# Local attention: the mask laid down by four products of 64 rows each, and GpSimd adding the halves of the squares

## The reference

```python
def local_attention(q, k, v):          # windows of 64 tokens, each looks at itself and the one before
    ...
    sim = jnp.einsum('bhwid,bhwjd->bhwij', bq, bk)          # bq is q * 8
    mask = (i < j) | (i > j + WINDOW) | (j == -1)
    sim = jnp.where(mask, -jnp.finfo(sim.dtype).max, sim)
    attn = jax.nn.softmax(sim, axis=-1)
    out = jnp.einsum('bhwij,bhwjd->bhwid', attn, bv)
...
def _layer(x, wqkv, qs, ksc, wo, lg, lb, w1, b1, w2, b2):
    h = shift_token(x)
    q, k, v = jnp.split(h @ wqkv, 3, axis=-1)               # 8 heads of 64
    q = l2norm(q) * qs
    k = l2norm(k) * ksc
    q, k = rotary_xpos(q, k)
    o = local_attention(q, k, v)
    x = x + o @ wo
    ...                                                     # then a gated feed-forward layer
```

## Time and profile before

| | before |
|---|---|
| median of 3 runs | 2363.22 us (2360.92 to 2367.59) |
| the profiled execution | 2362.19 us, of which its instructions span 2360.3 us |
| TensorE busy | 2103.0 us, 89% |
| VectorE busy | 1551.7 us, 66% |
| ScalarE busy | 1196.3 us, 51% |
| GpSimd busy | 518.5 us, 22% |
| granted TensorE clock, mean | 0.947 |

### The profile page before, as it was taken

The page is one execution under the profiler, slowest core; times in us unless marked ns, Lnnn a source line. Parts: engine busy times, 40 slices in busy tenths (PEclk is TensorE's granted clock), DMA queues, the critical chain, the costliest instruction groups (busy, mean ns, idle before and its releaser), DMA issues. The chain is left out here.

```text
span 2360.3 us, 40497 instructions
## 1 busy us (share of the span) xinstructions
PE 2103.0 (89%) x15567; PEld 1162.4 (49%) x15567; DVE 1551.7 (66%) x3059; ACT 1196.3 (51%) x2166; POOL 518.5 (22%) x836
## 2 busy tenths in 40 slices
PE   6998997896998998899699999989957957999999
PEld 3765665573765666345222222234535735455454
DVE  7986996557997896403788888540196777057650
ACT  4774773354775774311277777832143643242521
POOL 4431430213331440001643434000014110000000
PEclk9999999897999999999699999999978977999999
DMA  4000000001000000000311112000000110000000
GB/s 145 4 6 3 4 6 8 2 3 51 4 7 3 3 5 5 27 0 1 105 40 48 50 38 52 2 10 0 5 0 10 35 51 10 0 1 0 1 9 9
DMA packets 47682, 45.17 MB, mean 19 GB/s; under 512 B 33026, under 2 KB 37826, under 8 KB 46722
## 3 DMA queue, kind: packets, MB, share of 16 engines
q1 hardware_dynamic: 38386, 34.90, 4.8%
q0 software_dynamic: 9104, 7.68, 1.3%
HBM read 34.18 MB, written 4.46 MB: 16 GB/s over the span
## 5 line engine op out<-in xcount | busy, mean ns | idle before, releaser
L2310 DVE TENSOR_REDUCE fa_top<-psum 128x1 f32<-128x1024 f32 x256 | 299.4, 1217 | 44.3 <-PE psum L2209 44.3
L2286 ACT ACTIVATE fa_prob<-psum 128x512 f32<-128x512 f32 x512 | 275.2, 597 | 92.8 <-PE psum L2251 92.5
L758 POOL TENSOR_TENSOR turn_a<-turn_a,turn_b 128x1024 f32<-128x1024 f32 x64 | 151.4, 2365 | 268.3 <-DVE turn_b L978 268.3
L2177 POOL DMA_DIRECT2D area_a<-fa_parts_dram x240 | 133.2, 558 | 137.3 <-issue 137.0
L2251 PE MATMUL psum<-fa_stack_q,fa_stack_k 74*128 74x512 bf16 x512 | 156.9, 389 | 4.7 <-ACT fa_prob L2286 2.3
L549 DVE TENSOR_TENSOR scaled<-psum,area_b 128x512 f32<-128x512 f32 x8 | 5.5, 692 | 213.1 <-PE psum L518 213.1
L2264 PE MATMUL psum<-fa_prob,fa_pair_v 128*32 128x512 f32 x1024 | 137.2, 608 | 0.0
L775 PE MATMUL psum<-area_a,zt 128*128 128x512 f32 x256 | 129.5, 628 | 4.1 <-ACT zt L1193 2.7
L3601 PE MATMUL psum<-hidden_a,area_b 128*128 128x512 f32 x256 | 112.5, 592 | 0.0
L3601 PE MATMUL psum<-hidden_b,area_b 128*128 128x512 f32 x256 | 111.5, 592 | 0.0
L2207 PE MATMUL psum<-fa_stack_k,fa_stack_q 64*128 64x512 bf16 x256 | 87.2, 406 | 26.9 <-DVE fa_top L2310 19.9
(11 more groups left out here) (400 smaller groups left out, 4596.0 us busy)
## 6 DMA issues: line engine op xcount, KB each, us to landing
area_b<-in_L_ffn SPq DMA_DIRECT2D x2, 2888.0 KB, 9.7
fa_stack_q<-fa_parts_dram SPq DMA_DIRECT2D x144, 32.0 KB
fa_stack_k<-fa_parts_dram SPq DMA_DIRECT2D x144, 32.0 KB
area_a<-fa_parts_dram POOLq DMA_DIRECT2D x120, 32.0 KB, 2.3
fa_parts_dram<-fa_prob SPq DMA_DIRECT2D x12, 256.0 KB, 2.8
area_a<-in_L_ffn SPq DMA_DIRECT2D x1, 2482.0 KB, 18.1
moved_halves<-y SPq DMA_DIRECT2D x16, 127.0 KB
area_a<-fa_parts_dram POOLq DMA_DIRECT2D x120, 16.0 KB, 2.2
```

The source lines that it names most:

```text
L758: nc.gpsimd.tensor_tensor(turn_a[:], turn_a[:], turn_b[:], ALU.add).then_inc(rotary_sums.handle, 1)
L2177: pool.dma_start(to[at:at + D, :, :], parts_dram[b, which, pair[which]].rearrange("(h d) t -> d h t", d=D)[:, 2 * q:2 * q + 2, tokens]).th ...
L2286: nc.scalar.activation(prob[:, (2 * s + j) % RING, half * CHUNK:(half + 1) * CHUNK], slot_bank("scores", n), ACT.Exp, scale=float(D) ** -0 ...
L2310: nc.vector.tensor_reduce(top[:, g % 2, j, t:t + 1], psum[:, 2 * j:2 * j + 2, :].rearrange("p a n -> p (a n)"), AX.X, ALU.max, negate=True ...
```

## The change

Two edits in `l0_ffn`.

The squares: GpSimd gets a step `pool_square_halves`, ahead of `pool_rotary_sum` of the same tile, that waits for both halves of the squares and adds columns 32 to 63 of each head to columns 0 to 31, in place. VectorE's reduction waits for that (a new semaphore) in place of ScalarE's squares, and sums 32 columns a head, 512 in all, in place of 64 a head, 1024 in all.

The mask: in place of two products of 128 rows there are four of 64 rows by 64 columns, 512 columns moved each; the bank s gets both its halves from the rows 64 s to 64 s + 63 of the array, as the scores' products do. For that each half of the mask has to lie on either half of the partitions, so two of the 16 blocks of the SBUF copy hold the mask with its halves as they were, and the next two hold them exchanged; tile 0 and tile 8 take the first of each two, the other tiles the second. The one DMA of the masks becomes four on the same GpSimd queue, the same bytes in all but for which blocks are read, and TensorE waits for the four.

```diff
+    halved = core.sem("squares_halved")
+        def pool_square_halves(pool, l, n):
+            if not inside(n):
+                return
+            g = l * TILES + n
+            pool.wait_ge(*squared.at(2 * g + 2))
+            nc.gpsimd.tensor_tensor(squares[:, :, 0:D // 2], squares[:, :, 0:D // 2], squares[:, :, D // 2:], ALU.add).then_inc(halved.handle, 1)
...
+            kind = min(n % SEQ_TILES, 1)
             for s in range(2):
-                nc.tensor.matmul(score_banks[:, s, :], core.mask("ident"),
-                                 core.mask("local")[:, n * P:(n + 1) * P].unsqueeze(1).to_broadcast([P, H // 2, P]),
-                                 start=True, stop=False, skip_group_check=True)
+                for a in range(2):
+                    rows, block = slice(HALF * s, HALF * s + HALF), (0 if a == s else 2) + kind
+                    nc.tensor.matmul(score_banks[a * W:(a + 1) * W, s, :], core.mask("ident")[rows, rows],
+                                     core.mask("local")[rows, block * P:(block + 1) * P].unsqueeze(1).to_broadcast([HALF, H // 2, P]),
+                                     start=True, stop=False, skip_group_check=True)
...
-            dve.wait_ge(*squared.at(2 * g + 2))
-            nc.vector.tensor_reduce(square_sum[:, p], squares[:], AX.X, ALU.add).then_inc(summed_squares.handle, 1)
+            dve.wait_ge(*halved.at(g + 1))
+            nc.vector.tensor_reduce(square_sum[:, p], squares[:, :, 0:D // 2], AX.X, ALU.add).then_inc(summed_squares.handle, 1)
...
-                    pool.dma_start(core.masks[:], core.blobs["masks"]).then_inc(masks_there.handle, 16)
+                    here, before, behind = core.mask_at["local"][0], slice(0, HALF), slice(HALF, P)
+                    own, swapped, rest = slice(0, here + 2 * P), slice(here + 2 * P, here + 4 * P), slice(here + 4 * P, None)
+                    for to, rows, source in ((own, slice(0, P), core.blobs["masks"][:, own]), (rest, slice(0, P), core.blobs["masks"][:, rest]),
+                                             (swapped, before, core.blobs["masks"][behind, here:here + 2 * P]),
+                                             (swapped, behind, core.blobs["masks"][before, here:here + 2 * P])):
+                        pool.dma_start(core.masks[rows, to], source).then_inc(masks_there.handle, 16)
...
                     for n in range(TILES):
+                        pool_square_halves(pool, l, n)
                         pool_rotary_sum(pool, l, n)
                         pool_norm(pool, l, n)
...
-                        pe.wait_ge(*masks_there.at(16))
+                        pe.wait_ge(*masks_there.at(64))
```

More of the change, by code:

```diff
@@ L1477, in l0_ffn @@
             tally.done += 2 * TILES
+        halved.done += 2 * TILES
         first_cleared.done += BATCH
```

## The result

| | before | after |
|---|---|---|
| median | 2363.10 us (13 runs, 2360.07 to 2369.46) | 2355.86 us (13 runs, 2349.09 to 2360.49) |
| profiled execution (its span) | 2362.19 us (2360.3) | 2359.66 us (2357.9) |
| VectorE, GpSimd busy | 1551.7 and 518.5 us | 1523.6 and 601.7 us |
| steady period | 8.58 us | 8.42 us |

The ratio is 0.9969, 95% interval 0.9959 to 0.9979: 0.31% faster, right at the size that a measurement can tell. The forecast was 2355.8 us.

The account below looks back on a forecast made before the run. It took the loop over GpSimd to bound the steady attention; steady periods -5.1, tile 18 +1.2, attention ends -3.5 and start 0 gave -7.4 from 2362.2, so 2354.8, plus 1.0 for the median: 2355.8 us, range 2348 to 2364.

Parts of the forecast that it names:

- The loop over GpSimd sets the pace, not VectorE's load: Steady attention: the loop of GpSimd's rotary sum and norms with VectorE's norm and rotary products, 8.46 us, sets the period.
- It isn't in the loop: VectorE's reduction, 0.53 us shorter a tile, lies outside the loop over GpSimd and buys nothing directly.
- the forecast's second path: Steady tiles: shorter reduction starts `prob` 0.47 us earlier, copy L909 clears ScalarE before the logarithm; -5.1 us over 48 periods.
- The period that it falls to: Steady attention: period falls from 8.58 to 8.47 us, -5.1 us over 48 periods.
- Tile 18: GpSimd's addition and VectorE's L991 race for the SBUF port once an application: 0 to +2.5 us, taken as +1.2.
- The mask products: TensorE's four products run side by side, -0.2 us a tile, hidden in the steady loop behind GpSimd's loop.
- The ends: Last tiles of the four attentions: shorter reduction and two cheaper masks, -0.87 us each, -3.5 us in all.
- The start: Four mask DMAs, the last landing up to 3 us later: 0 to +1 us, taken together as 0.
- A: Rival: the four mask products don't overlap and TensorE becomes the bound; +11 us, 2374 us; chance 0.08.
- B: Rival: GpSimd's new addition takes the SBUF port from L991 in every tile; +60 us, 2420 us; chance 0.03.
- D: Rival: steady period stays at 8.58 us, only the attention ends gain, -3.5 + 1.2; 2361 us; chance 0.2.
- C: Rival: VectorE's load is the bound, steady period falls toward 8.0 us; -26 us, 2333 us; chance 0.05.

Follow-up runs that it names:

- half_before: Kernel before with k's half of the rotary sum on GpSimd left out: 2350.11 us, ratio 0.9942, steady period 8.585 us.
- split_before: Kernel before with GpSimd's rotary sum in two instructions, q's half started before k's products are done: 2353.32 us, ratio 0.9955, steady period 8.585 us.
- mask_only: Kernel before with only the mask's edit (four products, four DMAs): 2362.17 us, ratio 0.9989, steady period 8.50 us.
- half_after: Changed kernel with k's half of the rotary sum on GpSimd left out: 2338.82 us, ratio 0.9887, steady period 8.21 us.
- split_after: Changed kernel with GpSimd's rotary sum in two instructions, q's half started before k's products are done: 2338.26 us, ratio 0.9887, steady period 8.21 us.
- turn_wait: Changed kernel with GpSimd's new addition also waiting for VectorE's norm product of the tile before: 2355.36 us, ratio 0.9971, steady period 8.42 us.
- masks_first: Changed kernel with mask DMAs in order of need, the large rest last with its own semaphore: 2355.38 us, ratio 0.9965, steady period 8.42 us.
- half_squares: Kernel before with the squares' edit only and k's half of the rotary sum left out: 2342.3 us (one run), steady period 8.35 us.
- squares_only: Changed kernel with the mask as before (one DMA, two products): 2359.36 us, ratio 0.9978, steady period 8.42 us.

## Why the prediction was right or wrong

**The pace before: wrong.** "The loop over GpSimd sets the pace, not VectorE's load" failed by half_before and split_before: with GpSimd's loop 1.1 us shorter, the period stays at 8.585. The argument came from a tile at the start of layer 1, where GpSimd's loop was indeed all there was (8.47), and carried it over to the steady tiles. There the long loop had 8.585, VectorE's load 8.50 and GpSimd's loop 8.46. The late logarithm of the earlier trace rows was not a small delay on GpSimd's loop but a link of another loop, and the question not asked was what made the copy ahead of it late.

**The reduction: wrong place, right effect.** "It isn't in the loop" holds for GpSimd's loop only; in the long loop it stands once in two tiles. Its saving was as forecast (1.21 to 0.67 us, `prob` from 3.74 to 3.27 us after the sum), and the forecast's second path, over an earlier `prob` and an earlier copy L909, is in fact the long loop, told without its closing. That is why the number came near: whatever loop is named, the period falls until GpSimd's loop catches it.

**The period that it falls to: 8.42 in place of 8.47.** GpSimd takes up the rotary sum 108.35 - (107.59 + 0.68) = 0.08 us after the last product's end; in the steady tiles of the kernels without its addition this gap is 0.14 (mask_only: 98.76 + 0.68 to 99.58). 48 periods made -7.6 us for -5.1. That GpSimd's loop is the one that binds in after is shown by half_after and split_after.

**Tile 18: mechanism right, size at the upper end.** I took 1.2 us in all, between 0 and 2.5, as a race that either could win; GpSimd won it in both applications, 2.06 us. The mechanism is shown twice, by L1001's 2.32 us beside L739, and by the 1.23 us with turn_wait. The Trainium skill ("SBUF — State Buffer", "Who interferes with whom") has VectorE and GpSimd share a pair of ports for a whole instruction; these two rows agree with it.

**The mask products: size right, place wrong.** 0.59 to 0.41 us in duration and 0.25 us less of TensorE's time from start to start, for 0.2. By starts, the mask and the scores behind it take 0.34 us less (1.22 for 1.56), and the step into the mask 0.09 more. They are not hidden in the steady loop "behind GpSimd's loop", though: the mask stands in the long loop, and mask_only went from 8.58 to 8.50. Together with the squares that gain disappears under GpSimd's 8.42.

**The ends: right, a little small.** The four ends gave -4.2 for -3.5; the +0.3 in each step to tile 17, which the forecast didn't have, brings the sum to -3.6. In layer 0 of the first application each edit alone gave -0.47 and -0.55. The single ends scatter, from -0.2 to -1.9 us, which I can't take apart.

**The start: wrong.** Forecast 0 to +1, taken as 0; +3.0. I let the last of the four land at most 3 us after 22.6, in the shadow of the first scores at 28.9; it landed 5.5 us after. TensorE's first mask product, the one that waits, started at 28.15 and not at 25.52, the scores behind it took 1.92 us for 1.10, and VectorE had them later by as much. I had asked when VectorE wants the scores, and not how much TensorE has to do between mask and scores. masks_first took 1.92 us for the first scores without any wait, at a granted clock of 0.50, so that slowness is the clock's and not the wait's; in before the clock was back at full when they started (26.14). Against turn_wait and mask_only the order of the transfers is worth 1.3 to 1.8 us; up to 1.3 of after's 3.0 us are TensorE's slower stretch in that one execution. In the second application, where the masks lie there already, the start costs 0.3.

**The rivals.** A (masks one after the other) fell by 0.41 us for four. B fell in the steady tiles: L1001 (104.53, 1.23 us) is over 0.1 us before L739 starts (105.86), a closer call than the 1.7 us that the forecast spoke of; only tile 18 collides. D (ends alone) fell by the period. C was nearer the truth than its chance: VectorE's load was the second bound, 0.08 us beneath the first, and with the sum in two the period goes to 8.2; in the change itself GpSimd's loop stops it at 8.42. The number came out right by luck, since errors cancelled: -2.5 in the loops against +3.3 in the starts and +0.9 in tile 18, and the 1.6 us left are within the scatter of the medians.

## What to carry to other kernels

Where three engines take turns, list every closed loop, those that close only after two tiles as well, and give each its period: an alternating period (8.50, 8.68) is a sign of such a one, but a regular period doesn't exclude it (half_squares has 8.35 in every tile). A tile in which an engine is idle shows the loop that binds there, not the one in the steady state; the safe test is to shorten the suspected loop and see if the period moves. After an edit, the gain is the distance to the next loop below (here 0.16 of a possible 0.37 us), and an instruction put earlier on its engine puts all behind it later.

## What the runs showed of the hardware

- Two transfers of 32 KB on GpSimd's queue, issued behind one of 776 KB, landed after 17.8 us (median; 19.1 and 18.0 in mask_only and turn_wait); issued ahead of it, after 6.5 us.
- Two instructions of the kind that collide, started 0.01 us apart: GpSimd's addition took its usual 1.25 us, VectorE's product 2.32 in place of 1.23.
- Four bf16 products of 64 rows by 64 columns, 512 columns moved each, took 0.41 us, and two over the whole array 0.59, in steady tiles at the full granted clock. From the start of the mask products to that of the scores it is 0.24 us for 0.52. In masks_first, in a stretch of granted clock 0.50 (1.2 GHz), the four took 0.64 us.
- From the end of the last rotary product to GpSimd's one-piece sum it took 0.08 us where the new addition runs ahead of it (after, squares_only, half_after; idle 0.2 to 4.0 us) and 0.14 to 0.15 in nearly all tiles where it doesn't (before, mask_only, half_before; idle 4.0 us in the steady tiles; six at the starts have 0.08, at idle times of 0.7 to 8.4 us). What makes the difference stays open.
- At half the granted clock (0.50, turn_wait and mask_only from 24 to 30 us, masks_first at 26) TensorE took 1.92 us for the scores that take 1.04 in the steady tiles. In after they took 1.92 us too while the record of the granted clock says 1.00. The durations and the sister kernels speak against the record; why it differs stays open.
